# A vision block's weight preparation as steps of its attention program, with the orders of all engines written out for eight groups

## The chip, the cores and the metric

The kernel runs on one core of a Trainium2 chip. The metric is the device time of one execution in microseconds (us), the median of several runs. The core has five engines that run their own instruction streams and meet only at semaphores: PE (TensorE, matrix products and transposes), DVE (VectorE), ACT (ScalarE), POOL (GpSimd) and SP (SyncE, which here only issues DMAs). PE writes to PSUM, whose eight banks are held here in two tensors of four, `ps_s` and `ps_w`.

## The reference, cut to what matters

```python
h = tok(x)                       # 64 images of 3x112x112 -> 49 patches of 768 values
                                 #   rms norm, rounding to 8 bits, product with the token weight rounded to -1, 0, 1
                                 #   plus class token and position: h is 64 x 50 x 256
def attn(x):                     # x = layernorm(h); three scales, 16 heads of 16, causal
    for i in range(3):
        q, k, v = x @ Wq[i].T + bq[i], x @ Wk[i].T + bk[i], x @ Wv[i].T + bv[i]
        w = softmax(mask(q k^T * 4))
        o_i = layernorm((w v) @ Wo[i].T + bo[i]) * g[i] + b[i]
    return layernorm(concat(o_i) @ Wout.T + bout) * g2 + b2
h = h + attn(layernorm(h))
h = h + ffn(layernorm(h))        # gate and up 256 -> 704, silu, down 704 -> 256, all rounded to 8 bits
return h                         # the rounding steps of ffn are maxima over the WHOLE input
```

The maxima over the whole input mean that no FFN product can begin before the attention of the last image is done.

## The kernel before, in words

The program has three blocks, one after the other, each of which ends only when every engine has finished its part.

**Preparation (lines 303 to 510).** The weights are loaded into staging tensors (`tok_st`, `st_out`, `st_o`, `st_q`, `st_k`, `wv_sb`) and turned into what attention reads. The token weight is rounded and transposed (`tokT`). Wq and Wk are cut into a high part and a rest (`qk_hi`, `qk_lo`) so that PE can multiply them at a higher rate. Wo is centred (L417 to L421), transposed (L472), and multiplied with Wout (L487), so that one product later gives both the vector whose variance is wanted and the part of the final sum; this pair is `oy_hi`, `oy_lo`. The rows of biases (`brow_s`) are cut into three bf16 rows of `bias3` by a chain between ACT and POOL on one partition (L342 to L361). Nothing of the images is touched here.

**Attention (lines 697 to 1165).** The 64 images are eight groups of eight; a group is four pairs p = 0 to 3 of two images. The steps of a group are:

- for each pair: `sums` (the pair's largest value and sum of squares, L730 and L930), `scale`, `shift` (rounding, L744 and L950), `turn_q` (transposes, L1063 and L760), `embed` (token product, L1071, and statistics, L958 to L963), `norm_x` (L972), `turn_x` (transposes, L1078, and the copies `xh`, `xf` and the rest `xl`, L773 and L855);
- then, three scales each: `k` and `q` (L1087), `v` (L1104), `spread` (POOL lays k out by heads, L864), `scores` (L1125), `max`, `soft`, `sum`, `over` (the softmax), `turn_p` (L1139), `heads` (L1150), `project` (L1163), and `mix`, `mix2` (both layer norms of the end and the statistics for the FFN).

The first product `k` of a group needs the `xl` of all four pairs. `x_in` and `x_t` hold two pairs and one pair, so the load of pair 3 is issued once `x_q` of pair 1 has been written. The order on each engine is a table, `AT`: for each step its place in a round of 100 ticks, plus 100 for each round of lag behind the first steps. The same body is then run for every group (`round_parts`), with steps left out where the group does not exist. The four banks of `ps_w` go round in PE's order (`bank_plan`). Each step waits for what it needs, so the tables change only when things happen. The steps `sums`, `shift` and `turn_q` of the rounds after group 7 prepare the FFN's weights.

**FFN (lines 1229 to 1487).** It is the same in both kernels.

Of the kernel before, what the change touches and what calls it, by code (L numbers as in the profile page):

```python
# [14 lines left out]
F32 = mybir.dt.float32  # L15
# [52 lines left out]
ROUND = 100  # L68
AT = {
    "sp": {  # L70
        "sums": (0, 1, 2, 3,),
    },
    "act": {
        "sums": (9, 10, 29, 42,),
        "shift": (16, 22, 48, 62,),
# [11 lines left out]
        "sums": (1, 4, 18, 29,),
        "embed": (21, 36, 41, 51,),
        "turn_x": (50, 52, 54, 55,),
        "spread": (103, 105, 106, 108, 112, 113, 114, 119, 123, 125, 132, 140,),  # L90
        "sum": (115, 117, 120, 126, 130, 135, 139, 142, 148, 149, 207, 210,),
        "project": (131, 133, 137, 146, 147, 153, 200, 202, 209, 211, 227, 228,),
        "mix": (216, 222, 234, 238,),
        "mix2": (224, 243, 244, 245,),
    },
    "dve": {
        "sums": (3, 9, 25, 46,),
        "scale": (7, 12, 42, 62,),
        "shift": (10, 15, 53, 70,),
        "embed": (13, 36, 73, 92,),  # L100
        "norm_x": (81, 84, 90, 100,),
        "max": (114, 118, 126, 128, 138, 143, 149, 156, 169, 176, 182, 193,),
        "soft": (116, 119, 127, 130, 140, 147, 154, 161, 171, 177, 183, 202,),
        "sum": (122, 131, 134, 135, 144, 158, 164, 172, 174, 187, 191, 211,),
        "over": (129, 133, 137, 139, 148, 163, 167, 175, 178, 189, 204, 217,),
        "heads": (155, 157, 179, 188, 205, 232,),
        "project": (160, 165, 168, 185, 186, 201, 206, 208, 220, 223, 250, 252,),
# [31 lines left out]
USES_BANK = ("turn_q", "embed", "turn_x", "k", "q", "v", "turn_p", "heads", "project")


GU_CHUNKS = 2 * FC // 3


def round_parts(engine):

    body = engine_order(engine)

    def exists(step, i):
        m = i + step[-1]  # L150
        if step[0] in ("sums", "shift", "turn_q") and m >= GROUPS:
            return PAIRS * (m - GROUPS) + step[1] < (GU_CHUNKS + KC if step[0] == "sums" else GU_CHUNKS)
        return 0 <= m < GROUPS

    part = lambda i: [s for s in body if exists(s, i)]
    return [(0, part(0), 1), (1, part(1), 1), (2, body, GROUPS - 2)] + [(i, part(i), 1) for i in range(GROUPS, GROUPS + 4)]


def bank_plan():
# [4 lines left out]

    def fills(steps):
        return [(s, a) for s in steps if s[0] in USES_BANK for a in range(2 if s[0] == "turn_p" else 1)]

# [1364 lines left out]
```

## Time and profile before

| | us |
|---|---|
| median of 3 runs | 847.66 (845.89 to 847.9) |
| the profiled execution | 845.34 |
| its span in the trace | 843.5 |

The rows quoted further down come from that one profiled execution. Its span is 1.84 us shorter than its time. In a timeline row the first number is the start in us from the start of the span, the second the busy time of the row (neighbouring instructions of the same kind are merged, "xcount"), then engine, line, operation and tensors, and in brackets how long the engine had been idle and what ended that. PEclk is the clock that TensorE was granted, 1.00 being 2.4 GHz and 0.50 being 1.2 GHz.

### The profile page before, as it was taken

How to read it: one execution, taken by the hardware profiler on the slowest of the kernel's cores; microseconds unless marked ns; L12 is line 12 of the kernel's file. 1: busy time of each engine (PE TensorE's matmuls, PEld its weight loads, DVE VectorE, ACT ScalarE, POOL GpSimd, SP SyncE). 2: the span in 40 equal slices, each digit the busy share in tenths (PEclk: the TensorE clock that was granted, in tenths of full speed). 3: DMA queues.
4: the chain of work that ended last, by engine and by line, in shares of the span. 5: the costliest groups of instructions: out<-in, count | busy, mean ns of one | idle time of the engine just before them, and what ended most of it. 6: DMA issues, size and time to landing. Idle time of an engine off the chain costs nothing. (4 is left out here: it accounts for less than half of the span.)

```text
span 843.5 us, 28434 instructions
## 1 busy us (share of the span) xinstructions
PE 727.0 (86%) x11302; PEld 576.0 (68%) x11302; DVE 648.5 (77%) x1362; ACT 512.0 (61%) x1078; POOL 535.1 (63%) x806
## 2 busy tenths in 40 slices
PE   2603799999999999999999999999999999367665
PEld 0402678887888878878888877888788877234354
DVE  6535586688879887987898798879886985758847
ACT  0444566675676666666666766676666665278673
POOL 0062685596779678966977696789678763521154
PEclk9855699999999999999999999999999999879968
DMA  7001001000000000000001000000001010000004
GB/s 248 0 28 44 30 17 32 2 31 17 19 14 19 17 17 31 3 18 16 31 2 32 2 32 17 17 17 17 21 19 37 2 37 3 1 1 0 0 25 132
DMA packets 14963, 22.05 MB, mean 26 GB/s; under 512 B 1972, under 2 KB 11446, under 8 KB 14839
## 3 DMA queue, kind: packets, MB, share of 16 engines
q1 hardware_dynamic: 14402, 19.91, 7.6%
q8 instruction: 89, 1.46, 0.7%
q10 hardware_dynamic: 436, 0.40, 0.2%
q14 instruction: 36, 0.29, 0.1%
HBM read 17.03 MB, written 3.28 MB: 24 GB/s over the span
## 5 line engine op out<-in xcount | busy, mean ns | idle before, releaser
L864 POOL TENSOR_TENSOR k_bd<-kT,rmask 128x400 f32<-128x400 f32 x192 | 166.2, 891 | 13.8 <-ACT kT L780 13.1
L873 POOL TENSOR_TENSOR prob<-prob,rsum 128x400 f32<-128x400 f32 x96 | 118.6, 1235 | 20.5 <-DVE rsum L997 20.4
L810 ACT COPY pT<-ps_w 128x400 f32<-128x400 f32 x192 | 86.6, 507 | 40.4 <-PE ps_w L1139 39.8
L1139 PE MATMUL ps_w<-pack,prob 128*128 128x128 f32 x768 | 102.6, 277 | 1.8 <-POOL prob L873 1.0
L1104 PE MATMUL ps_w<-wv_sb,xf 128*50 128x128 f32 x1536 | 98.9, 272 | 0.0
L1139 PEld LDWEIGHTS ps_w<-pack,prob 128*128 128x128 f32 x768 | 84.9, 141 | 18.0 <-issue 11.2
L1163 PE MATMUL ps_w<-oy_hi,o_hi 128*128 128x512 f32 x192 | 93.8, 489 | 0.0
L795 ACT COPY v_bd<-ps_w 50x512 f32<-50x512 f32 x96 | 55.7, 581 | 47.0 <-PE ps_w L1104 45.8
L824 ACT ACTIVATE ps_w<-ps_w 128x256 f32<-128x256 f32 x96 | 35.4, 369 | 80.1 <-PE ps_w L1163 79.9
L1104 PEld LDWEIGHTS ps_w<-wv_sb,xf 128*50 128x50 f32 x1536 | 78.0, 125 | 0.3
L802 ACT ACTIVATE prob<-prob 128x400 f32<-128x400 f32 x96 | 68.0, 708 | 15.6 <-DVE prob L985 15.5
L878 POOL TENSOR_TENSOR ln<-ln,ln_eps 128x1 f32<-128x1 f32 x96 | 19.0, 198 | 92.0 <-ACT ps_w L824 92.0
L981 DVE TENSOR_REDUCE nmax<-ps_s 128x16 f32<-128x400 f32 x96 | 72.6, 757 | 5.8 <-PE ps_s L1125 5.2
L1163 PE MATMUL ps_w<-oy_lo,o_hi 128*128 128x512 f32 x192 | 76.0, 396 | 0.0
L1163 PE MATMUL ps_w<-oy_hi,o_lo 128*128 128x512 f32 x192 | 75.6, 394 | 0.0
L985 DVE TENSOR_TENSOR prob<-ps_s,nmax 128x400 f32<-128x400 f32 x96 | 74.0, 771 | 1.1
L992 DVE TENSOR_REDUCE rsum<-prob 128x16 f32<-128x416 f32 x96 | 73.5, 773 | 1.3 <-ACT prob L802 1.2
L1087 PE MATMUL ps_w<-xh,qk_hi 128*128 128x400 f32 x192 | 70.6, 368 | 1.7 <-POOL xl L855 1.7
L1125 PE MATMUL ps_s<-k_bd,qT 64*25 64x200 f32 (+1 forms) x3072 | 70.5, 291 | 0.0
L1087 PE MATMUL ps_w<-xl,qk_hi 128*128 128x400 f32 x192 | 67.0, 349 | 0.0
L1087 PE MATMUL ps_w<-xh,qk_lo 128*128 128x400 f32 x192 | 66.7, 348 | 0.0
L1013 DVE SCALAR_TENSOR_TENSOR acc<-ps_w,ln,acc 128x256 f32<-128x256 f32 x64 | 30.9, 482 | 42.9 <-POOL ln L880 33.7
(214 smaller groups left out, 1766.6 us busy)
## 6 DMA issues: line engine op xcount, KB each, us to landing
x_in<-in_x SPq DMA_DIRECT2D x64, 147.0 KB
out<-hidden SPq DMA_DIRECT2D x16, 200.0 KB
tok_st<-in_tok_w SPq DMA_DIRECT2D x1, 768.0 KB, 7.2
st_out<-in_wout SPq DMA_DIRECT2D x1, 768.0 KB, 5.2
st_o<-in_wo SPq DMA_DIRECT2D x1, 768.0 KB, 7.0
st_q<-in_wq SPq DMA_DIRECT2D x1, 768.0 KB, 8.7
st_k<-in_wk SPq DMA_DIRECT2D x1, 768.0 KB, 10.1
wv_sb<-in_wv SPq DMA_DIRECT2D x1, 768.0 KB, 10.3
```

The costliest lines, as they stand in the source:

```text
L802: nc.scalar.activation(pr, pr, ACT.Exp).then_inc(exp_ready, 1)
L810: nc.scalar.copy(pT[:, s % 2, 4 * a:4 * a + 4, :, e * LQ:(e + 1) * LQ], ps_w[:, bank].rearrange("p (j t) -> p j t", j=4)[:, :, 0:QB * LQ]. ...
L864: last = nc.gpsimd.tensor_tensor(k_bd[:, v % KBD, c], kT[:, w % 2, c, 2 * p * L:(2 * p + 2) * L].unsqueeze(1).broadcast_to([P, HR, 2 * L]) ...
L873: nc.gpsimd.tensor_tensor(pr, pr, rsum[:, s % 2, e, 1].unsqueeze(2).broadcast_to([P, H, WIDTH[e]]), ALU.mult).then_inc(prob_ready, 1)
L981: nc.vector.tensor_reduce(top, s_ps, AX.X, ALU.max, negate=True).then_inc(max_ready, 1)
L985: nc.vector.tensor_tensor(prob[:, s % 2, e, :, 0:WIDTH[e]].rearrange("p (r h) t -> p r h t", r=2), s_ps, top.unsqueeze(3).broadcast_to([P, ...
L992: nc.vector.tensor_reduce(rsum[:, s % 2, e, 0], prob[:, s % 2, e, :, 0:WIDTH[e] + 1], AX.X, ALU.add).then_inc(sum_ready, 1)
L1087: mm = nc.tensor.matmul(G[:, 0:GT], wt[:, w, q, k, c * P:(c + 1) * P], xt[:, k], start=(t == 0), stop=(t == 3 * KC - 1))
L1104: mm = nc.tensor.matmul(G[row:row + L, cols], xf[:, k, tokens], wv_sb[:, w, k, e], start=False, stop=(k == KC - 1), skip_group_check=True)
L1125: mm = nc.tensor.matmul(ps_s[32 * b:32 * b + LQ, e, r, c * HR * W:(c + 1) * HR * W], qT[rows, w % 2, c, first:first + LQ], k_bd[rows, v % ...
L1139: mm = nc.tensor.transpose(G[:, j * P:(j + 1) * P], flat[:, (4 * a + j) * P:(4 * a + j + 1) * P], pack[:])
L1163: mm = nc.tensor.matmul(G[:], ot[:, s % 2, c, 2 * (p % 2):2 * (p % 2) + 2].rearrange("p b t -> p (b t)"), wt[:, w, c], start=False, stop=( ...
```

## The change

The block of preparation is gone. Its operations are now steps in the tables of the attention block (`tok_sum`, `tok_turn`, `beta`, `y_scale`, `o_centre`, `wo_turn`, `fold`, `k_hi`, `q_lo`, `v_cut`, `z_cut` and more), placed among the steps of group 0. The first two pairs of images are issued right behind the token weight and the identity, ahead of all other weights. Since preparation and attention now live at the same time, the staging tensors are laid into tensors that are used late: `st_out`, `st_o`, `st_q` and `woT` into `hidden` from slot 8 on (group 2 and later), `st_k` into `k_bd`, the token weight into `pT`, the bias rows into `wgT`, `wdT` and `acc`.

Four operations move to another engine: the scaled shift of the token weight from DVE to ACT, the copies of `tokT` from DVE to ACT (two instead of six), the rest of Wk from DVE to POOL, and the memsets from DVE to POOL. The bias cut is made in two pieces, one for v (768 values) and one for the output (1536 values), instead of 2304 values at once. `AT` now lists a tick for each step of each of the eight groups, so groups may differ in order; `round_parts`, `Part` and the loop of SP are gone. Waits are added where a step of attention first needs something prepared (`qk_cut` before `k` and `q`, `v_cut` before `v`, `o_cut`, `fold_lo` and `z_cut` before `project`, `tok_copied` before `embed`, `fold_lo` before group 2's `embed`).

```diff
-    with nc.Block() as block:
-        @block.sync
-        def _(sp):
-            sp.dma_start(tok_st[:], tok_w.rearrange("(k p) n -> p k n", p=P)).then_inc(loads["tok"], 16)
...
-    prep.close()
+    st_out, st_o, st_q = (hidden[:, 8 + 6 * j:14 + 6 * j] for j in range(3))
+    woT = hidden[:, 26:32].rearrange("p a (b t) -> p (a b) t", t=P).rearrange("p (s d e) t -> p s d e t", s=NS, d=KC)
...
+                if kind == "weights" and step[1] == 1:
+                    sp.dma_start(st_q, weight_rows(wq)).then_inc(loads["wq"], 16)
+                    sp.dma_start(st_k, weight_rows(wk)).then_inc(loads["wk"], 16)
...
+                if kind == "k_lo":
+                    pool.wait_ge(split_k, 1)
+                    nc.gpsimd.tensor_tensor(qk_lo[:, :, 1], by_row(st_k), qk_hi[:, :, 1].bitcast(F32), ALU.subtract).then_inc(qk_cut, 1)
...
+                if kind == "q_lo":
+                    dve.wait_ge(split_q, 1)
+                    nc.vector.tensor_tensor(qk_lo[:, :, 0], by_row(st_q), qk_hi[:, :, 0].bitcast(F32), ALU.subtract).then_inc(qk_cut, 1)
...
+                if kind == "fold":
+                    s = step[1]
+                    pe.wait_ge(scaled_y, 1)
+                    pe.wait_ge(wo_copied, s + 1)
+                    wait_released(pe, step)
...
                 if kind in ("k", "q"):
                     w, c, q = *step[1:3], int(kind == "k")
                     pe.wait_ge(xl_ready, PAIRS * (m + 1))
+                    pe.wait_ge(qk_cut, 2)
...
                     pe.wait_ge(o_lo_ready, S * m + s + 1 + AHEAD)
+                    pe.wait_ge(o_cut, 1)
+                    pe.wait_ge(fold_lo, NS)
+                    pe.wait_ge(z_cut, 3)
...
-ROUND = 100
...
+    "pe": {
+        "tok_mean": (0,),
+        "turn_q": (1, 4, 8, 9, 25, 38, 60, 68, 92, 111, 128, 144, 163, 175, 194, 214, 240, 260, 275, 290, 307, 322,
```

**SP, from its first instruction.** `x_in` is the buffer of images, L623 in the changed kernel; the four loads of the first two pairs now stand third. In the kernel before, SP reads:

```order
L306 DMA tok_st<-in_tok_w 128x2x768
L307 DMA id<-in_ident 128x128
...
L313 DMA st_q<-in_wq 128x6x256
L313 DMA st_k<-in_wk 128x6x256
L314 DMA wv_sb<-in_wv 128x6x256
L303 UNCONDITIONAL_BRANCH
L698 UNCONDITIONAL_BRANCH
L714 DMA x_in<-in_x 49x768 x16
```

and in the changed kernel:

```order
L591 DMA pT<-in_tok_w 128x2x768
L592 DMA id<-in_ident 128x128
L623 DMA x_in<-in_x 49x768 x4
...
L601 DMA hidden<-in_wq 128x6x256
L602 DMA k_bd<-in_wk 128x6x256
L604 DMA wv_sb<-in_wv 128x6x256
L605 DMA pT<-in_brow 1x768
L606 DMA hidden<-in_wout 128x6x256
L607 DMA hidden<-in_wo 128x6x256
L608 DMA acc<-in_brow 1x1024
L623 DMA x_in<-in_x 49x768 x60
```

The first two pairs moved from behind everything to the front; pairs 2 and 3 of group 0 are the first of the sixty loads behind the weights.

**PE, up to the first product `k` of group 0** (`xh` with `qk_hi`). The kernel before has, after its block of preparation:

```order
L1063 MATMUL ps_w<-id,x_q 128x128 x6
L1071 MATMUL ps_w<-tokT,x_qT 128x256 x6
L1063 MATMUL ps_w<-id,x_q 128x128 x6
L1078 MATMUL ps_w<-id,x_t 128x128 x2
L1071 MATMUL ps_w<-tokT,x_qT 128x256 x6
L1078 MATMUL ps_w<-id,x_t 128x128 x6
L1087 MATMUL ps_w<-xh,qk_hi 128x400
```

The changed kernel has:

```order
L1247 MATMUL ps_w<-tokT,x_qT 128x256 x12
L1185 MATMUL ps_w<-hidden,bcol 1x256 x6
L1238 MATMUL ps_w<-id,x_q 128x128 x12
L1247 MATMUL ps_w<-tokT,x_qT 128x256 x6
L1220 MATMUL ps_w<-ybias,ones 128x256
L1214 MATMUL ps_w<-ones,wgT 128x1 x6
L1255 MATMUL ps_w<-id,x_t 128x128 x2
L1247 MATMUL ps_w<-tokT,x_qT 128x256 x6
L1255 MATMUL ps_w<-id,x_t 128x128 x6
L1229 MATMUL ps_w<-hidden,bo_col 1x256 x6
L1265 MATMUL ps_w<-xh,qk_hi 128x400
```

`beta` (L1185), `y_spread` (L1220), `bo_turn` (L1214) and `bo_fold` (L1229) moved in among the transposes and token products of group 0. `wo_turn` and `fold` stand further down, behind the first scores.

**DVE, between the last shift of group 0 and the first maximum** (`nmax`). The changed kernel has, among group 1's first steps:

```order
L957 TENSOR_TENSOR qk_lo<-hidden,qk_hi 128x3x512
L1029 TENSOR_REDUCE xs<-x_in 128x1
...
L1049 TENSOR_SCALAR x_q<-x_t 128x768
L967 TENSOR_REDUCE o_mean<-hidden 128x6
L969 TENSOR_SCALAR o_mean<-o_mean 128x6
L971 TENSOR_TENSOR hidden<-hidden,o_mean 128x1536
L1085 TENSOR_REDUCE nmax<-ps_s 128x16 x2
```

In the kernel before, the same work (`st_o` and `o_mean`) stands in the block of preparation:

```order
L417 TENSOR_REDUCE o_mean<-st_o 128x6
L419 TENSOR_SCALAR o_mean<-o_mean 128x6
L421 TENSOR_TENSOR st_o<-st_o,o_mean 128x1536
L426 TENSOR_REDUCE b_mean<-brow_st 1x3
L428 TENSOR_SCALAR b_mean<-b_mean 1x3
```

The centring of Wo and the rest of Wq moved to where DVE formerly waited for the first scores.

## Rows read from the trace of the kernel before

**Rows 1.** The page: the span, and PE's clock in 40 slices.
```profile
span 843.5 us, 28434 instructions
...
PEclk9855699999999999999999999999999999879968
```

**Rows 2.** Windows: busy us (and count) by engine, clock, DMA share, GB/s.
```profile
40.00:50.00 10.00, 0.00 (x0) 0.00 (x0) 4.83 (x1) 6.69 (x4) 4.54 (x1) 0.65 0.00 0
...
180.00:260.00 80.00, 79.72 (x1349) 65.40 (x1349) 67.76 (x153) 51.88 (x117) 61.60 (x99) 1.00 0.06 18
```

**Rows 3.** Waits of PE, 93 to 720 us: total us, times, longest.
```profile
PE ps_s L1116 <- POOL k_bd L864: 1.7, 6, 0.5
PE ps_s L1116 <- DVE prob L985: 1.4, 2, 1.2
```

**Rows 4.** Timeline: the token weight is taken up; the first images are asked for.
```profile
7.99 1.75 DVE L376 TENSOR_REDUCE tok_sum<-tok_st 128x2 f32<-128x1536 f32 x1 [5.06 <-DMA tok_st<-in_tok_w]
...
58.56 15.78 SPq L714 DMA_DIRECT2D x_in<-in_x  x8
```

**Rows 5.** Timeline: group 0 from its first image to its first scores.
```profile
62.38 0.84 ACT L730 ACTIVATE x_t<-x_in 128x768 f32<-128x768 f32 x1 [4.08 <-DMA x_in<-in_x]
...
73.13 0.56 DVE L950 TENSOR_SCALAR x_q<-x_t 128x768 bf16<-128x768 f32 x1
...
77.41 0.84 ACT L730 ACTIVATE x_t<-x_in 128x768 f32<-128x768 f32 x1 [1.98 <-DMA x_in<-in_x]
...
93.00 0.70 PE L1087 MATMUL ps_w<-xh,qk_hi 128*128 128x400 f32 x1 [1.71 <-POOL xl L855]
...
102.97 0.26 PE L1116 MATMUL ps_s<-mask,pick 64*128 64x200 bf16 x2
```

**Rows 6.** DMA: a window of the weights; images alone, 58 to 80 us.
```profile
10.00:20.00 10.00, 4.91 (x14) 1.76 (x14) 7.94 (x23) 0.43 (x3) 0.00 (x0) 0.96 1.09 354
```
```profile
GB/s 0 0 56 101 179 162 184 162 162 78 11 0 0 30 0 0 0 0 0 0 0 123 106 128 168 22 0 0 0 0 84 134 151 173 6 0 0 0 0 0
```

**Rows 7.** Timeline: operations of preparation that move into attention.
```profile
12.52 4.35 PE L465 MATMUL ps_w<-st_out,bcol 128*1 128x256 f32 x12 [1.88 <-DMA st_out<-in_wout]
...
16.98 1.66 DVE L414 TENSOR_SCALAR st_out<-st_out,gcol 128x256 f32<-128x256 f32 x6 [1.18 <-PE ps_w L465]
...
22.31 0.93 DVE L426 TENSOR_REDUCE b_mean<-brow_st 1x3 f32<-1x768 f32 x1
...
22.54 2.79 PE L472 MATMUL ps_s<-id,st_o 128*128 128x128 f32 x12 [5.67 <-DVE st_o L421]
...
28.21 5.40 PE L487 MATMUL ps_s<-st_out,woT 128*128 128x256 f32 x24
...
33.54 1.49 PE L495 MATMUL ps_s<-one_row,brow_s 1*128 1x1 f32 x12
...
35.50 1.89 PE L505 MATMUL ps_w<-st_out,bo_col 128*1 128x256 f32 x8
...
39.65 2.11 ACT L342 CAST bias<-brow_s 1x2304 bf16<-1x2304 f32 x1 [5.41 <-DVE brow_s L452]
41.67 1.47 ACT L344 CAST qk_hi<-st_k 128x1536 fp32r<-128x1536 f32 x1
```

**Rows 8.** Timeline: the same subtraction on DVE, alone and beside POOL.
```profile
35.15 1.75 DVE L444 TENSOR_TENSOR qk_lo<-st_q,qk_hi 128x1536 fp32r<-128x1536 f32 x1
...
41.84 4.54 POOL L359 TENSOR_TENSOR brow_r<-brow_s,bias 1x2304 f32<-1x2304 f32 x1 [39.72 <-ACT bias L342]
43.16 4.83 DVE L454 TENSOR_TENSOR qk_lo<-st_k,qk_hi 128x1536 fp32r<-128x1536 f32 x1 [3.55 <-ACT qk_hi L344]
```

**Rows 9.** Timeline: the end of attention and the first FFN instruction.
```profile
724.08 0.39 PE L1158 MATMUL ps_w<-bias,ones 96*128 96x512 bf16 x1 [1.29 <-DVE o_lo L1003]
...
735.61 0.17 DVE L1045 COPY stat<-ln 128x4 f32<-128x4 f32 x1
...
736.86 1.28 ACT L1242 ACT_TABLE_LOAD   x1 [8.86 <-PEq L697]
```

More of the change, by code:

```diff
@@ L85 @@
     },
     "pool": {
[L87 to L94, printed above, removed]
+        "sums": (0, 1, 2, 3, 16, 17, 28, 36, 57, 59, 69, 78, 109, 114, 121, 137, 168, 172, 184, 186, 221, 227, 236,
+            259, 281, 291, 303, 305, 338, 339, 353, 365,),
@@ L100 @@
[L100 to L107, printed above, removed]
@@ new lines @@
+        "fold": (53, 54, 55,),
+        "heads": (56, 57, 74, 80, 102, 115, 123, 127, 145, 146, 174, 185, 201, 202, 215, 219, 246, 261, 262, 277,
+            284, 295, 320, 321, 346, 347, 358, 365, 386, 403, 413, 424, 425, 436, 455, 470, 480, 492, 503, 507, 534,
+            540, 552, 561, 570, 577, 587, 588,),
+        "project": (61, 62, 63, 64, 93, 96, 97, 98, 113, 114, 124, 126, 134, 135, 136, 137, 156, 157, 158, 159, 180,
[4 rows of a table added]
+    },
+}
+PER_GROUP = {
+    "sums": PAIRS, "scale": PAIRS, "shift": PAIRS, "turn_q": PAIRS, "embed": PAIRS, "norm_x": PAIRS, "turn_x": PAIRS,
+    "mix": PAIRS, "mix2": PAIRS, "k": NS * KC, "q": NS * KC, "v": S, "heads": S, "spread": V, "project": V,
+    "scores": U, "max": U, "soft": U, "sum": U, "over": U, "turn_p": U,
@@ L139 @@
[L139 to L156, printed above, removed]
@@ L191, in layer @@
+USES_BANK = ("tok_mean", "tok_turn", "beta", "wo_turn", "fold", "bo_turn", "y_spread", "bo_fold",
+             "turn_q", "embed", "turn_x", "k", "q", "v", "turn_p", "heads", "project")
+def bank_plan():
+    order = [(step, a) for step in engine_order("pe") if step[0] in USES_BANK for a in range(2 if step[0] == "turn_p" else 1)]
+    return {key: (n % NBANK, n // NBANK + 1, order[n - NBANK] if n >= NBANK else None) for n, key in enumerate(order)}
 def layer(nc, x, tok_w, cls, pos, wq, wk, wv, wo, bq, bk, brow, ln_g, ln_b, wout, ln2_g, ln2_b,
@@ L668, in layer, with walk @@
+    def walk(engine, do):
+        for step in engine_order(engine):
+            do(step)
     HALVES = ((0, 0), (ROWB, 1))
@@ L720, in _ @@
         def _(act):
-            def do(step, part):
-                kind, m = step[0], part.group(step)
+            for dst, src in ((token0, pos), (g2, ln2_g), (b2, ln2_b)):
+                act.dma_start(dst[:], src.broadcast_to([P, D])).then_inc(loads["small"], 16)
+            act.wait_ge(pool_up, 1)
+            for row in (0, ROWB):
+                act.dma_start(cls_st[row:row + 1], cls).then_inc(loads["small"], 16)
+            act.wait_ge(set_up, 1)
+            act.sem_inc(pt_read, AHEAD)
```

937 lines of the change are left out of this document (534 added, 403 removed), and 69 rows, old and new, of the table AT.

## The prediction

> **What bounds the kernel now.** I read the page's slices first, then windows of the stages, PE's waits, and last the timelines at the two ends of attention. Three stretches appear. Up to about 93 us PE is mostly idle: in the window from 40 to 50 us it does nothing while ACT, DVE and POOL cut bias rows [rows 2], and its clock is at the lower level in slices 3 and 4 [rows 1]. From then on PE is busy 79.72 of 80 us in a window of the middle, with DVE at 67.76 as the next [rows 2], and its waits from 93 to 720 us are a few of up to 1.2 us [rows 3]: this stretch lasts as long as PE has work. Last, attention drains and the FFN follows: its first instruction stands at 736.86 us [rows 9], and from there to the end of the span, 843.5 [rows 1], is 106.6 us of code that the change leaves alone.
>
> So the time is the start of the first product `k` (93.00 us [rows 5]), plus PE's work, plus drain and FFN. I call that start T. The change pays by moving T forward, and costs by what it adds to PE's work behind T, and by waits that new orders open.
>
> **T before.** The first images are asked for when preparation is over, at 58.56 us [rows 4]. The first pair is taken up at 62.38 [rows 5]. Pair 3 can only be loaded once pair 1's `x_q` is written, at 73.13 + 0.56 = 73.69, and is taken up at 77.41, 3.7 us later; from there to T it is 93.00 - 77.41 = 15.6 us of a chain from engine to engine [rows 5].
>
> **T after, the data.** Pairs 0 and 1 are issued behind the token weight, pairs 2 and 3 behind all weights. Ahead of pair 2 on the queue stand the token weight and five more loads of 768 KB, 64 KB of identity, 384 KB of broadcast rows (from ACT's queue) and 588 KB of the first two pairs: 5.64 thousand KB, or 5.8 MB. Weights came at 354 GB/s [rows 6], which makes 16.4 us; with a start at about 4 us that is 20. Images do not come at that rate: loaded alone they moved 162 to 184 GB/s at the most [rows 6]. For the first two pairs that costs 3.5 us instead of 1.7, for pairs 2 and 3 (another 588 KB) 3.5 us. Pair 3 is then there at about 25 us, not before 23. The condition of before (`x_q` of pair 1 plus 3.7 us) lies earlier: the token weight is there at 7.99 us [rows 4], and two pairs through `sums`, `scale` and `shift` take 73.69 - 62.38 = 11.3 us [rows 5], which gives 8 + 11.3 + 3.7 = 23.
>
> The Trainium skill (DMA: Bandwidth & Descriptors, Why a DMA increments its semaphore by 16 and not by 1) says that a load is spread over the largest number of engines up to 16 that divides its slowest dimension, so 49 rows would go to 7 of 16. The trace agrees: 7/16 of 354 GB/s would be 155. The same page (Queues, rings and completion order) has descriptors taken in ring order on each engine, so that pairs 2 and 3 would wait for the weights. No row of before has images queued behind weights. If that rule did not hold here, pair 3 would come at 23 us, and T and the time would be 2 us less.
>
> **T after, what is put into the chain.** From the landing of pair 3 to T the tables now also have, on PE, `beta` 4.35, `bo_turn` 1.49 and the larger part of `bo_fold` 1.89 = 7.7 us; on DVE the centring of the bias rows (two operations of some 0.93) and `y_scale` 1.66 = 3.5 us; on ACT two casts of 1.47 and three bf16 cuts of 768 values, one third of 2.11 each, = 5.0 us [rows 7]. Together 16.2 us. All exposed would be the upper bound, none (hidden in the waits of the chain, as the 1.98 us of ACT before pair 3 or the 1.71 us of PE before `k` [rows 5]) the lower. `bo_fold` stands right ahead of `k` and is nearly bare, `beta` stands ahead of two transposes that pairs 2 and 3 need; the casts of ACT stand between `sums` and `shift`. I take half, 8.1 us. `q_lo`, 1.75 us alone [rows 8], runs on DVE while PE, ACT and POOL finish the last `turn_x`, and I cost it at nothing; bare it would be 1.75.
>
> The rest of Wk moves to POOL. DVE's subtraction of 128x1536 took 1.75 us alone and 4.83 us when it began during POOL's operation, which ended at 41.84 + 4.54 = 46.38: up to that moment 3.2 us, and then its own 1.6 [rows 8]. So DVE stood still while POOL worked. POOL's `k_lo` and `v_left` now run beside DVE's part of the chain. I add 1.5 us for it, between 0 and 3.1. The Trainium skill (SBUF — State Buffer, SBUF: two separate sides) states this as a rule against such a mix: the port pair that GpSimd shares with VectorE is held for a whole instruction, and the other blocks. The trace agrees; by it alone, every POOL subtraction of the preparation would cost DVE up to its full length.
>
> T after = 25 + 15.6 + 8.1 + 1.5 = 50.2 us, 42.8 us earlier. Bounds: 23 + 15.6 + 2 = 41, and 27 + 15.6 + 16.2 + 1 = 60.
>
> **PE's work behind T.** `wo_turn` (2.79) and `fold` (5.40) [rows 7] now stand among scores and products of group 0, where PE is full, so they cost 8.2 us in whole. At the full clock throughout the transposes may take 1 us less. All other products are the same in number and shape. PE begins `k` at the lower clock as before, so that term cancels.
>
> **New waits behind T.** DVE has `o_centre` right ahead of the first maximum. In the kernel before the first scores come 102.97 - 93.00 = 10 us after T [rows 5], and in that time DVE now has `q_lo` and some 8 us of work; `o_centre` ends about 11 us after T. The last rows of `bias3` hang on a chain of ACT and POOL, and `fold_lo` on ACT and DVE; `project` waits for all of them, behind `fold`, `heads` and `v`. POOL has 3 us of subtraction in the middle of the spreads (1536 of 2304 values, 4.54 us [rows 8]). I take 2 us in all. Above, one such subtraction bare and a late `project` give 8 (3.0, and the 5.40 of `fold` once more as the time by which its rest could be late [rows 7]); below, the waits of 1.7 and 1.4 us [rows 3] could vanish in the new orders, -3.
>
> **The drain.** Before, PE's last two projections begin at 724.08 and the last statistics end at 735.78 [rows 9], 11.7 us. The new order transposes the last four probabilities in one go, then does both heads, then the last four projections, so four pairs instead of two go through `mix` and `mix2` after PE, which makes DVE's tail longer; but PE has about 10 us more work left behind the last scores, and waits less for them. I set the sum at nothing, plus or minus 3.
>
> **The sum.** 845.34 - 42.8 + 8.2 + 2 = 812.7 us for an execution like the profiled one. The median of the runs of before lies 2.3 us above that execution; I add 1.3 and predict 814.
>
> **The rivals.**
> 1. The start pays in full: DVE's and PE's additions hide in the idle parts, T is 41 to 45, and orders per group take away the small waits of PE. 845.3 - 50 + 8.2 - 2 = 801.5. For it: the chain of before has waits on each engine [rows 5] in which additions can hide. Against: the three additions stand on three different engines of one chain. From 796 to 805.
> 2. The start stays late: preparation is then itself the chain, as a walk with the additions bare, T 57 to 62. 845.3 - 34 + 8.2 + 5 = 824.5. This is also the case that the change does not do what it says: `k` waits for the preparation, not for the images. For it: ACT, PE and DVE each do the preparation in series with the images. From 820 to 832.
> 3. The new orders take PE's cover away in every group, and the kernel gets slower. The tables now pair the steps (two maxima, then two exponents). The scores of a bank wait until DVE has read the last ones; the longest such wait was 1.2 us [rows 3]. There are six pairs of scores in each of eight groups, 48 places. At 1.2 us in each it costs 58 us, and the time is 845.3 - 42.8 + 10.2 + 58 = 871. It decides from 32.6 / 48 = 0.68 us at each place. Against it: DVE is busy 67.76 of 80 us [rows 2], which leaves 12 us in each group, so that a table would have to be placed badly for it.
>
> **How the numbers follow.** The forecast, 805 to 820, has a chance of 0.6; rival 1, 0.17; rival 2, 0.17; rival 3 in full 0.03, and in part (a gain of which less than half is left, 832 to 845) 0.03. The range reaches to both sides until about 0.2 is out: 799 to 827. About 0.3% is what a measurement of this kernel can tell from no change, 2.5 us here. Faster by over that: 0.96; within it: 0.01; slower: 0.03.
>
> **What would show each step.** In the profile after, the first product `k` stands at about 50 us; the fourth `sums` of ACT begins at about 25 us after a wait for the DMA of `x_in`; PE in the stretch behind T is as dense as before, but for `fold`, whose rows add 8 us between T and the start of the FFN: attention then takes 737 - 93 + 10 = 654 us from T on. FFN is 107 us in both. The prediction is wrong if the fourth `sums` comes later than 28 us (the data), if from there to T it is more than 32 us (the chain), or if T to the start of the FFN is over 662 us or under 647 (the orders).

## The result and the profile after

| | before | predicted | after |
|---|---|---|---|
| median of the runs (4 and 4) | 847.78 | 814 (799 to 827) | 819.58 (819.25 to 823.28) |
| profiled execution | 845.34 | 812.7 | 819.57 |
| fourth `sums` of ACT begins | 77.41 | 25 | 28.97 |
| from there to the first product `k` (T) | 15.6 | 25.2 | 26.8 |
| T | 93.00 | 50.2 | 55.75 |
| T to the first FFN instruction | 643.9 | 654 | 656.4 |
| from there to the end of the span | 106.6 | 106.6 | 105.5 |

All in us. The ratio of the runs is 0.9683, with a 95% interval of 0.9654 to 0.9712: faster, by 27 us (28 between the medians). The rows account for the profiled executions: T came 37.2 us earlier, attention from T on took 12.5 us longer, the FFN 1.1 us less, together 25.8 us, and the two executions differ by 25.77. The median is inside the range, 5.6 us above the number. The profiled execution is 6.9 us above its own number: T is 5.5 late, the stretch from T to the FFN 2.4 longer than forecast, the FFN 1.1 shorter.

The page after: the span, and PE's clock in 40 slices, which answers to [rows 1].
```profile
span 817.7 us, 28887 instructions
...
PEclk9869999999999999999999999999999999679979
```

The timeline after, from the load of Wo to the first product `k`, which answers to [rows 5, 7]. First the start in us, then the busy time.
```profile
14.75 2.06 SPq L607 DMA_DIRECT2D hidden<-in_wo  x1
...
28.97 0.84 ACT L707 ACTIVATE x_t<-x_in 128x768 f32<-128x768 f32 x1 [0.74 <-DMA x_in<-in_x]
...
33.52 3.43 POOL L834 TENSOR_TENSOR qk_lo<-k_bd,qk_hi 128x1536 fp32r<-128x1536 f32 x1
...
35.23 1.74 DVE L979 TENSOR_SCALAR b_mean<-b_mean 1x3 f32<-1x3 f32 x1
...
36.90 1.63 POOL L841 TENSOR_TENSOR pT<-pT,bias 1x768 f32<-1x768 f32 x1
37.04 2.30 DVE L981 TENSOR_TENSOR wgT<-acc,b_mean 1x768 f32<-1x768 f32 x1
...
39.27 0.54 DVE L1049 TENSOR_SCALAR x_q<-x_t 128x768 bf16<-128x768 f32 x1
...
42.93 2.55 PE L1214 MATMUL ps_w<-ones,wgT 1*128 1x1 f32 x12
...
45.90 1.49 PE L1247 MATMUL ps_w<-tokT,x_qT 128*128 128x256 bf16 x6
...
50.45 2.28 DVE L957 TENSOR_TENSOR qk_lo<-hidden,qk_hi 128x1536 fp32r<-128x1536 f32 x1
...
51.07 2.12 POOL L864 TENSOR_TENSOR xl<-xf,xh 128x200 fp32r<-128x200 f32 x1
51.20 4.32 PE L1229 MATMUL ps_w<-hidden,bo_col 128*1 128x256 f32 x12
...
55.75 0.45 PE L1265 MATMUL ps_w<-xh,qk_hi 128*128 128x400 f32 x1 [0.23 <-POOL xl L864]
```

The rows show three things. Pair 3 is taken up at 28.97, waited for until then. Between the `shift` of pair 3 on ACT (which ends at 34.03) and its `x_q` on DVE at 39.27 stands only the centring of the bias rows, and two of its operations take 1.74 and 2.30 us while POOL subtracts. At the end `xl`, 0.60 us elsewhere, takes 2.12 beside DVE's `q_lo`; four `xl` and the additions between them then end just where `k` begins.

Behind T, in group 0, POOL begins a subtraction (`z_left`) 0.4 us before DVE's `x_q` of group 1's second pair. What follows, on POOL, DVE and PE:
```profile
68.96 3.10 POOL L841 TENSOR_TENSOR wgT<-wgT,bias 1x1536 f32<-1x1536 f32 x1
...
69.35 5.42 DVE L1049 TENSOR_SCALAR x_q<-x_t 128x768 bf16<-128x768 f32 x1
...
79.86 1.09 PE L1194 MATMUL ps_w<-id,hidden 128*128 128x128 f32 x4 [2.75 <-DVE hidden L1062]
```

Windows of the start of `k` before (93 to 100 us) and after (55.75 to 62.75), and of the stretch behind the wait. Columns: PE, PEld, DVE, ACT, POOL busy, then the granted clock.
```profile
93.00:100.00 7.00, 7.00 (x27) 6.96 (x28) 2.61 (x7) 3.50 (x7) 3.07 (x5) 0.66 0.00 0
```
```profile
55.75:62.75 7.00, 6.48 (x38) 6.17 (x39) 5.83 (x11) 4.61 (x7) 7.00 (x9) 1.00 0.00 1
```
```profile
75.00:80.00 5.00, 1.86 (x53) 1.20 (x48) 4.77 (x10) 4.30 (x7) 4.38 (x6) 0.83 0.19 60
80.00:85.00 5.00, 5.00 (x45) 3.42 (x46) 4.87 (x10) 3.91 (x7) 2.43 (x3) 0.50 0.02 3
```

`x_q` takes 5.42 instead of 0.56 us, `embed` on DVE is late, the bank that `wo_turn` wants is late, PE idles 2.75 us, and then its clock is at the lower level (1.2 GHz) for five microseconds. At T it is the other way round: before, PE had idled 1.71 us ahead of `k` and ran it at the lower level for two thirds of 7 us; after, PE is busy with `bo_fold` until 0.23 us ahead of `k`, and `k` runs at 2.4 GHz at once. The end, PE's last product and the first FFN instruction, first before:
```profile
727.10 0.39 PE L1163 MATMUL ps_w<-oy_hi,o_lo 128*128 128x512 f32 x1
```

and after:
```profile
698.88 0.39 PE L1350 MATMUL ps_w<-oy_hi,o_lo 128*128 128x512 f32 x1
...
712.16 1.28 ACT L1429 ACT_TABLE_LOAD   x1 [11.69 <-PEq L588]
```
From the end of PE's last projection to the first FFN instruction it is 12.9 us, where it was 9.4.

### The profile page after: what moved, and what is told of

Its sections match the earlier page's. It is cut to its first block and busy times, and to the rows that moved or that the text cites. A ratio compares the mean times of both kernels' runs of the same rounds, so it can differ in the third digit from the quotient of the medians.

```text
span 817.7 us, 28887 instructions
## 1 busy us (share of the span) xinstructions
PE 728.1 (89%) x11302; PEld 573.7 (70%) x11302; DVE 649.7 (79%) x1346; ACT 519.0 (63%) x1085; POOL 544.5 (67%) x817
## 5 line engine op out<-in xcount | busy, mean ns | idle before, releaser
L1323 PE MATMUL ps_w<-pack,prob 128*128 128x128 f32 x768 | 95.1, 275 | 1.8 <-DVE hidden L1062 0.9
L891 POOL TENSOR_TENSOR ln<-ln,neg_half 128x1 f32<-128x1 f32 x96 | 53.4, 557 | 7.5
```

Of the source, the lines that this page charges most:

```text
L1323: mm = nc.tensor.transpose(G[:, j * P:(j + 1) * P], flat[:, (4 * a + j) * P:(4 * a + j + 1) * P], pack[:])
```

## The experiments

The first four were timed side by side, then four, two and two more, each lot with the kernel before on the same chip (846.11, 846.05, 846.66 and 847.92 us). "T to FFN" is from the first product `k` to the first FFN instruction in the profiled execution. Where steps move, a table `MOVES` is added which `engine_order` applies: each entry is a step and the step that it now stands behind.

| run | median us | ratio, interval | fourth `sums` | T | T to FFN |
|---|---|---|---|---|---|
| c0_after | 820.58 | 0.9696 (0.9671 to 0.9721) | 28.98 | 55.75 | 655.9 |
| e1_data | 815.53 | 0.9630 (0.9601 to 0.9659) | 26.67 | 53.45 | 655.9 |
| e2_klo | 821.48 | 0.9698 (0.9671 to 0.9726) | 28.83 | 55.80 | 658.5 |
| e3_zleft | 821.25 | 0.9683 (0.9657 to 0.9710) | 29.35 | 56.13 | 659.1 |
| e4_fold_twice | 824.86 | 0.9735 (0.9711 to 0.9759) | 29.14 | 55.92 | 660.9 |
| e5_before_x | 848.01 | 1.0012 (0.9998 to 1.0027) | 77.70 | 93.79 | |
| e6_behind | 823.61 | 0.9733 (0.9708 to 0.9757) | 29.37 | 52.56 | 663.8 |
| e7_tail | 816.97 | 0.9660 (0.9635 to 0.9684) | 29.01 | 55.91 | 651.5 |
| e8_rests | 815.41 | 0.9633 (0.9619 to 0.9648) | 29.15 | 55.28 | 650.0 |
| e9_best | 814.36 | 0.9619 (0.9606 to 0.9633) | 29.60 | 54.12 | 651.5 |
| e10_chain | 810.26 | 0.9557 (0.9539 to 0.9575) | 26.35 | 50.55 | 653.6 |
| e11_data_rests | 812.98 | 0.9593 (0.9576 to 0.9610) | 26.20 | 51.61 | 654.8 |

**The changed kernel again.**

> The changed kernel once more, as a reference for the runs beside it on the same chip. Theory and rival alike expect 819.6 us (within 2.5), the first product k at 55.75 us, the fourth sums of ACT at 28.97 us, the first FFN instruction at 712.2 us.

It reproduced the rows shown above within 0.1 us up to 75 us, the 5.4 us of `x_q` included (5.41), and T to FFN within 0.5. The wait of 2.75 us came again, but the lower clock behind it was shorter: 0.66 from 80 to 85 us, that is 3.4 us at half speed, where it had been 0.50 throughout.

**Weights behind the images.**
```diff
-        "weights": (2, 3, 4,),
+        "weights": (2, 3, 4, 6.5,),
...
+                if kind == "weights" and step[1] == 3:
+                    sp.dma_start(st_o, weight_rows(wo)).then_inc(loads["wo"], 16)
+                    sp.dma_start(wv_sb[:].rearrange("p s k e n -> p (s k) (e n)"), weight_rows(wv)).then_inc(loads["wv"], 16)
```

> The loads of Wo and Wv (1.5 MB) move on the DMA queue behind the images of pairs 2 and 3. Theory (the images of pair 3 are late by 4 us because they stand behind all weights in the queue, and the whole chain up to T starts with them): 1.5 MB at 354 GB/s are 4.4 us; the fourth sums of ACT begins at about 24.5 instead of 28.97 us, T at 51.3 instead of 55.75, time 815.2. Rival 1 (the images are late for another reason, such as their issue after x_q of pair 1): the fourth sums stays within 1 us of 28.97 and the time at 819.6. Rival 2 (data are early but the chain is bound by ACT, DVE and POOL work of the preparation): the fourth sums moves by 4 us and T by less than 2, time above 817.6.

The timeline of that run, ACT and PE:
```profile
24.96 0.80 ACT L738 COPY x_qT<-ps_w 128x768 bf16<-128x768 bf16 x1 [2.33 <-DVE ln L1066]
...
26.67 0.84 ACT L708 ACTIVATE x_t<-x_in 128x768 f32<-128x768 f32 x1
...
53.45 0.45 PE L1266 MATMUL ps_w<-xh,qk_hi 128*128 128x400 f32 x1 [0.78 <-POOL xl L865]
```
The fourth `sums` moved by 2.3 us and T by exactly as much, so the chain from there on is rigid, and both rivals fall. But 4.4 us had been expected. `sums` no longer waits for a DMA: it stands on ACT behind the copy `x_qT` of pair 1, which waits for pair 0's statistics. So the data were worth 2.3 us, and the next bound, the work of the first two pairs, stood right behind them. The profiled executions differ by 2.1 us (816.34 against 818.48), the medians by 5.0. The intervals of the two ratios just fail to overlap, so part of the rest may be real; it has no row in the trace, and its cause stays open.

**The rest of Wk on DVE.**
```diff
-        "k_lo": (6,),
...
+        "k_lo": (29.5,),
```

> The rest of Wk (k_lo, 128x1536) is subtracted on DVE right behind q_lo instead of on POOL at 33.5 us. Theory (DVE stands still beside POOL's subtraction, so b_centre's second and third operation take 1.74 and 2.30 us instead of 0.17 and 0.95, and x_q of pair 3 waits for them): those two fall to below 2.0 us together, x_q of pair 3 is written 1.5 to 2.9 us earlier than at 39.27, and T comes 1.5 us earlier at 54.2, if k_lo's 1.75 us on DVE hide beside the rest of bo_fold. Time 818.1. Rival (the long operations of DVE have another cause): the two stay at about 4 us and T at 55.75 or later, by up to 1.75.

The timeline of DVE, POOL and PE:
```profile
36.94 0.94 DVE L981 TENSOR_TENSOR wgT<-acc,b_mean 1x768 f32<-1x768 f32 x1
37.81 0.54 DVE L1049 TENSOR_SCALAR x_q<-x_t 128x768 bf16<-128x768 f32 x1
...
51.19 2.16 DVE L954 TENSOR_TENSOR qk_lo<-k_bd,qk_hi 128x1536 fp32r<-128x1536 f32 x1
...
51.69 2.24 POOL L863 TENSOR_TENSOR hidden<-hidden,b 128x256 f32<-128x256 f32 x1
...
55.80 0.45 PE L1265 MATMUL ps_w<-xh,qk_hi 128*128 128x400 f32 x1 [1.73 <-POOL xl L861]
```
The subtraction moved to DVE with its step. That of `b_centre` fell from 2.30 to 0.94 us, and `x_q` came 1.5 us earlier, so POOL's work did hold DVE. Its other operation stayed long (1.77), beside `v_left`. The gain did not reach T: `k_lo` on DVE now holds POOL's addition (0.73 elsewhere) for 2.24 us among the `xl`, and PE waits for them. The same 1.5 us were paid at the other end, from DVE to POOL. The expected 54.2 for T and 818.1 for the time failed.

**The first subtraction of the output rows later.**
```diff
+MOVES = {
+    "pool": ((('z_left', 0, 0), ('sum', 3, 0)),),
+}
```

> POOL's first subtraction of the output bias rows (1x1536, 3.10 us at 68.96) moves behind its first four normalisations of probabilities, some 15 us later. Theory (x_q of group 1's second pair, 0.56 us alone, took 5.42 us at 69.35 because POOL's operation held DVE, all of DVE and the bank of embed came late, PE stood idle for 2.75 us and then ran from 80 to 85 us at the lower clock): x_q takes less than 2.6 us, PE has no wait over 1 us between 70 and 90 us and no stretch at the lower clock there, and the time from T to the FFN falls from 656.4 to about 652, time 815.6. Rival (the wait comes from the order of the steps on PE and DVE): x_q gets shorter, but the wait and the lower clock stay, time 819.6.

DVE, POOL and PE:
```profile
69.71 0.88 DVE L1059 TENSOR_SCALAR x_q<-x_t 128x768 bf16<-128x768 f32 x1
...
83.90 3.10 POOL L851 TENSOR_TENSOR wgT<-wgT,bias 1x1536 f32<-1x1536 f32 x1
...
84.28 2.74 DVE L1068 TENSOR_TENSOR xs<-xs,tok_unit 128x1 f32<-128x1 f32 x1
...
88.82 0.26 PE L1309 MATMUL ps_s<-mask,pick 64*128 64x200 bf16 x2 [2.21 <-issue]
...
99.95 0.92 PE L1344 MATMUL ps_w<-pT,v_bd 128*32 128x50 f32 x64 [1.94 <-DVE oy_lo L1009]
```
`x_q` took 0.88 us and PE was busy all of 70 to 80 us: the wait of 2.75 us and the lower clock behind it were gone, as expected. But nothing was left of it at the end (T to FFN 659.1), and the expected absence of any wait over 1 us up to 90 us failed. The subtraction now held an operation of one column for 2.74 us and stood ahead of two spreads (86.97 to 88.62), and PE's scores came behind them, after 2.2 us of idling for which the profile names no releaser. At 99.95 PE waited 1.94 us more for a late `oy_lo`, and its clock was 0.66 from 100 to 105 us. In group 1, PE idled another 1.60 us at 203.35, again without a releaser. So the holding of `x_q` is shown, and the expected 815.6 failed, since the subtraction did other harm at its new place.

**`fold` twice.**
```diff
-                    for k in range(KC):
+                    for k in (0, 1, 0, 1):
                         for kk in range(KC):
                             mm = nc.tensor.matmul(G[:, k * D:(k + 1) * D], woT[:, s, kk, k], st_out[:, s * KC + kk],
```

> PE makes the products of fold twice (24 more matrix products of 128x256, same result). Theory (work of PE behind T is bare, so what the change added there costs its full length): the row of fold grows from 5.3 to 10.6 us and the time by 5.3, to 825.4 against 820.1 for the changed kernel. Rival (behind T there is slack, and added work of PE partly disappears in waits that exist anyway): the time grows by less than 3 us.

The row of `fold` grew from 5.34 to 10.52 us, T to FFN by 5.0 us, the median by 4.3. Work of PE behind T is bare.

**The kernel before with its first images loaded at once.**
```diff
+            sp.wait_ge(x_clear, 1)
+            for p in (0, 1):
+                for row, b in ((0, 0), (ROWB, 1)):
+                    sp.dma_start(x_in[row + 1:row + L, p, :], x[2 * p + b]).then_inc(x_loaded[p], 16)
             for n in ("wk", "wv"):
```

> The kernel before, with one part of the change alone: the images of the first two pairs are loaded behind the weights during the preparation, not after it. Theory (they only spare their own landing; the rest of the gain comes from preparation running beside group 0): the first sums of ACT begins at 58.7 instead of 62.38 us, T at 89.3 instead of 93.00, time 843.6 less than 1 us off, against 847.3 for the kernel before (ratio 0.996). Rival (loading at once is the main part): T falls by 10 us or more.

ACT and DVE:
```profile
59.57 0.84 ACT L737 ACTIVATE x_t<-x_in 128x768 f32<-128x768 f32 x1 [0.47 <-PEq L305]
...
65.38 0.95 DVE L937 TENSOR_REDUCE xs<-x_in 128x1 f32<-128x768 f32 x1 [3.75 <-POOL prob L901]
```
and in the kernel before:
```profile
64.58 0.95 DVE L930 TENSOR_REDUCE xs<-x_in 128x1 f32<-128x768 f32 x1 [3.76 <-POOL prob L894]
```
The first `sums` on ACT came 2.8 us earlier, and T did not move forward (93.79). The images were not what group 0 waited for longest: in both kernels DVE's first reduction waits for POOL's memsets at the start of the attention block. This part alone is worth nothing here; the gain needs the preparation and group 0 to overlap. No run has the overlap without the early images.

**The centring, `bo_turn` and `bo_fold` behind T.**
```diff
+MOVES = {
+    "pe": ((('bo_turn', 0, 0), ('q', 1, 0, 0)), (('bo_fold', 0, 0), ('bo_turn', 0, 0)), (('bo_fold', 1, 0), ('bo_fold', 0, 0)),),
+    "dve": ((('b_centre', 0, 0), ('q_lo', 0, 0)), (('bo_col', 0, 0), ('shift', 0, 1)), (('z_row', 0, 0), ('bo_col', 0, 0)), (('z_row', 1, 0), ('z_row', 0, 0)),),
+}
```

> The centring of the bias rows, bo_turn and bo_fold (DVE 5.0 us as measured, PE 2.6 and 4.3 us) move behind the first products k and q; y_scale, the casts and POOL's subtractions stay. Theory (these stand bare in the chain from the images to T: x_q of pair 3 waits 4.9 us for the centring, embed of pair 3 waits 2 us for bo_turn): x_q of pair 3 at 34.4 instead of 39.27 us, T at 48.8 instead of 55.75, and 3 to 4 us of it are given back behind T where PE is full, so T to the FFN is 659 to 660 instead of 656.2, time 816.7. Rival (POOL is the real chain: its subtraction k_lo, v_left and the memset of prob end at 40.9 us, and its work on the second layer norm comes behind them): x_q of pair 3 is early, but T stays at 53 or later and the time is 820 or more.

DVE and PE, and the window behind T:
```profile
35.94 1.82 DVE L1060 TENSOR_SCALAR x_q<-x_t 128x768 bf16<-128x768 f32 x1 [1.21 <-ACT x_qT L748]
...
52.56 0.70 PE L1276 MATMUL ps_w<-xh,qk_hi 128*128 128x400 f32 x1 [5.20 <-POOL xl L875]
...
62.13 2.75 PE L1240 MATMUL ps_w<-hidden,bo_col 128*1 128x256 f32 x12 [0.30 <-issue]
```
```profile
52.56:59.56 7.00, 7.00 (x27) 6.95 (x28) 4.26 (x11) 3.13 (x5) 5.20 (x7) 0.67 0.00 1
```
T came 3.2 us earlier, not 7: `x_q` was itself held beside `k_lo` (1.82 us), and POOL kept the rest. And 7.9 us came back behind T: the moved products (`bo_turn` 1.49, `bo_fold` 2.75), and a start of `k` at the lower clock (0.67 over 7 us, 2.3 us lost), with PE idle for 5.20 us ahead of it. The run was 3 us slower than the changed kernel. What stands ahead of `k` on PE, in the shadow of POOL's `xl`, costs nothing there, and `k` behind it started at the higher level.

**The end in the order of before.**
```diff
+    "pe": ((('heads', 4, 7), ('turn_p', 9, 7)), (('project', 8, 7), ('turn_p', 10, 7)), (('project', 9, 7), ('project', 8, 7)),),
...
+    "dve": ((('mix', 0, 7), ('project', 8, 7)), (('project', 9, 7), ('mix', 0, 7)), (('heads', 5, 7), ('project', 9, 7)), (('mix', 1, 7), ('heads', 5, 7)),),
```

> The last group's end in the order of the kernel before: the heads and projections of the fifth scale half (pairs 0 and 1) come ahead of the last transposes and heads. Theory (four pairs instead of two go through both layer norms on DVE after PE's end, and DVE is full from there on): DVE's first sum of the last four begins 1.2 us earlier than at 695.91, PE's end to the first FFN instruction falls from 12.9 us towards the 9.4 of before, time 2 to 3 us less than the changed kernel's 820.1. Rival (the drain is the same sum of work in either order): within 1 us of 820.1.

POOL and DVE in group 0, and the end:
```profile
68.60 0.88 DVE L1062 TENSOR_SCALAR x_q<-x_t 128x768 bf16<-128x768 f32 x1
...
69.03 3.43 POOL L854 TENSOR_TENSOR wgT<-wgT,bias 1x1536 f32<-1x1536 f32 x1
...
697.53 0.39 PE L1363 MATMUL ps_w<-oy_hi,o_lo 128*128 128x512 f32 x1
...
707.41 1.28 ACT L1442 ACT_TABLE_LOAD   x1 [8.29 <-PEq L601]
```
```profile
690.00:697.90 7.90, 5.87 (x81) 4.25 (x82) 6.06 (x18) 1.91 (x7) 3.23 (x8) 0.78 0.01 3
```
The drain is 9.5 us again, as before, but from the first `k` of group 7 to the FFN it is 102.8 us against 101.7: what the drain gave, PE's stretch ahead of it took. From that `k` to PE's end PE idled 3.4 us, where it had idled 0.9, and its last 8 us ran at a clock of 0.78. The rival holds for the end. The 3.6 us of the median come from elsewhere. In this execution, with not one step of group 0 changed, `x_q` happened to start 0.43 us ahead of `z_left`; it took 0.88 us, the wait of PE did not arise, and group 0 took 69.2 instead of 74.4 us. The runs of this kernel lie from 814.19 (the profiled one) to 819.99. PE's wait of 2.75 us stands in the traces of after, c0_after, e1_data, e2_klo, e4_fold_twice and e6_behind (2.74), and not in this one. That the same near tie decides the runs without a trace is likely and not shown.

**All subtractions on DVE.**
```diff
-        "k_lo": (6,),
-        "v_left": (7, 18,),
-        "z_left": (24, 37,),
...
+MOVES = {
+    "dve": ((('k_lo', 0, 0), ('q_lo', 0, 0)), (('v_left', 0, 0), ('norm_x', 0, 0)), (('v_left', 1, 0), ('sums', 1, 1)), (('z_left', 0, 0), ('soft', 5, 0)), (('z_left', 1, 0), ('max', 7, 0)),),
+    "act": ((('z_cut', 2, 0), ('fold_hi', 2, 0)),),
+}
```

> All five subtractions that cut weights and bias rows (k_lo, v_left twice, z_left twice) run on DVE, none on POOL; nothing else moves. Theory (a subtraction on POOL and work on DVE hold each other, and whether group 0 loses 4 to 5 us depends on which of the two starts first, z_left or the x_q of DVE): the operations of b_centre take 0.2 and 1.0 us instead of 1.74 and 2.30, x_q of group 1's second pair less than 1.5 us instead of 5.42, PE has no wait over 1 us between 60 and 95 us, T at 54 to 56 us (k_lo now ends beside POOL's xl), T to the FFN 651 to 653 instead of 656, time 815 and without two levels among the runs. Rival (DVE is full in this stretch, so 7 us more work on it cost more than the holding did): T to the FFN stays at 655 or more, time 819 or more.

DVE's centring, `x_q`, and PE's window:
```profile
35.41 0.16 DVE L990 TENSOR_SCALAR b_mean<-b_mean 1x3 f32<-1x3 f32 x1
35.64 0.94 DVE L992 TENSOR_TENSOR wgT<-acc,b_mean 1x768 f32<-1x768 f32 x1
...
67.99 0.88 DVE L1060 TENSOR_SCALAR x_q<-x_t 128x768 bf16<-128x768 f32 x1
```
```profile
75.00:80.00 5.00, 5.00 (x65) 4.24 (x63) 4.97 (x8) 4.87 (x10) 3.08 (x3) 1.00 0.01 3
```
The rows came as expected: 0.16 and 0.94, 0.88, no wait of PE over 0.7 us from 60 to 95 us, T 55.28, T to FFN 650.0, median 815.41. DVE has some 8 us more work and the kernel is 5 us faster than the changed one. `x_q` of pair 3 came at 36.52 instead of 39.27, and T gained only 0.5 us of that: beside `q_lo` and `k_lo` on DVE an `xl` took 2.12 and an addition 2.24 us on POOL. Only the spread of the runs (812.57 to 817.24) did not shrink.

**The chain rearranged, twice.** Both have the edits of e1_data and e8_rests, and all four `xl` of group 0 ahead of the additions to `hidden`. The first of the two also put POOL's memsets ahead of the work on the images, `k_hi` and `k_lo` into the pause before pair 3, `q_lo` and the centring behind `embed` and `norm_x`, and `bo_turn` behind the last `embed`.
```diff
+    "dve": ((('k_lo', 0, 0), ('embed', 0, 0)), (('y_row', 0, 0), ('shift', 3, 0)), (('norm_x', 0, 0), ('y_row', 0, 0)), (('b_centre', 0, 0), ('norm_x', 0, 0)), (('q_lo', 0, 0), ('embed', 2, 0)), (('y_scale', 0, 0), ('norm_x', 3, 0)), (('bo_col', 0, 0), ('norm_x', 3, 0)), (('v_left', 0, 0), ('norm_x', 0, 0)), (('v_left', 1, 0), ('sums', 1, 1)), (('z_left', 0, 0), ('soft', 5, 0)), (('z_left', 1, 0), ('max', 7, 0)),),
...
+    "pool": ((('clear', 0, 0), ('sums', 1, 0)), (('clear', 1, 0), ('clear', 0, 0)), (('clear', 2, 0), ('clear', 1, 0)),),
```

> As the run with all subtractions on DVE, and in addition: the loads of Wo and Wv behind the images, k_hi and k_lo in the pause before the third pair's images, the memsets early, q_lo and the centring where DVE waits for PE, bo_turn behind the last embed, and all four xl ahead of the additions to hidden. Theory (the holding and the bare steps of the chain from the images to T can be had back): fourth sums of ACT at 26.7 us, from there to T 20 to 22 us instead of 26.8, T at 47 to 49, T to the FFN 651 to 654, time 807 to 811. Rival (what leaves one engine of the chain shows on the next, as with the centring moved alone): T at 51 or later, time 813 or more.

```profile
15.09 1.80 POOL L837 MEMSET v_bd<- 128x2048 f32 x1
...
15.83 4.50 DVE L938 CAST id<-id 128x128 bf16<-128x128 f32 x1
```
T was 54.12 and not 47 to 49: the cast of the identity, 0.22 us in c0_after, took 4.50 us beside the memsets, and everything behind it moved back by 3.4 us. So the second put them elsewhere:
```diff
+    "dve": ((('k_lo', 0, 0), ('embed', 0, 0)), (('q_lo', 0, 0), ('embed', 1, 0)), (('y_row', 0, 0), ('shift', 3, 0)), (('norm_x', 0, 0), ('y_row', 0, 0)), (('b_centre', 0, 0), ('embed', 2, 0)), (('v_left', 0, 0), ('norm_x', 3, 0)), (('bo_col', 0, 0), ('norm_x', 3, 0)), (('y_scale', 0, 0), ('norm_x', 3, 0)), (('v_left', 1, 0), ('z_row', 1, 0)), (('z_left', 0, 0), ('soft', 5, 0)), (('z_left', 1, 0), ('max', 7, 0)),),
+    "act": ((('k_hi', 0, 0), ('small', 0, 0)), (('q_hi', 0, 0), ('sums', 3, 0)), (('v_cut', 0, 0), ('turn_q', 3, 0)), (('v_cut', 1, 0), ('sums', 1, 1)), (('z_cut', 2, 0), ('fold_hi', 2, 0)),),
+    "pool": ((('clear', 0, 0), ('embed', 1, 0)), (('clear', 1, 0), ('turn_x', 3, 0)),),
+    "pe": ((('bo_turn', 0, 0), ('embed', 3, 0)),),
```

> As the run with every step rearranged, but the memsets of POOL stand again behind the first images' work (ahead of them they shifted x_q of pair 1 from 20.1 to 23.5 us), q_hi and q_lo move into pauses of ACT and DVE ahead of x_q of pair 3, the centring into the pause between the last two embeds. Theory (memsets on POOL held DVE's clipping of the token weight, and the rest of the chain was moved back with it): x_q of pair 1 at 20.5, the fourth sums at 26.7, T at 49 to 51, T to the FFN 650 to 652, time 807 to 810. Rival (the chain gives nothing more): T at 53 or later, time above 812.

```profile
45.45 5.18 PE L1244 MATMUL ps_w<-hidden,bo_col 128*1 128x256 f32 x12 [1.46 <-DVE bo_col L1009]
...
50.55 0.45 PE L1280 MATMUL ps_w<-xh,qk_hi 128*128 128x400 f32 x1
```
T is 50.55, in the expected 49 to 51, the median 810.26: 0.9557 of the kernel before, the best of all, where the changed kernel had 0.9696 in c0_after. T to FFN was 653.6 and not 650 to 652; 1.60 us of it are idling of PE in group 1 (at 191.89) for which the profile names no releaser. `k` now follows `bo_fold` without a pause, 4.9 us behind the last `xl` (45.69), so `bo_fold` is the next bound.

> Two edits together: the loads of Wo and Wv behind the images, and all subtractions on DVE. Theory (the two are independent: the one moves the start of the chain by 2.3 us, the other frees group 0 of the holding): the fourth sums at 26.7, T at 53.0, T to the FFN 650, time 812.9 or 2.3 less than with the subtractions alone. Rival (they share their gain): time as with the subtractions alone, 815.

The window behind T:
```profile
51.61:58.61 7.00, 7.00 (x30) 6.95 (x30) 3.11 (x12) 3.51 (x6) 3.96 (x6) 0.76 0.00 0
```
The median is 812.98, as the sum of the two said. In the trace T moved by 3.7 us against e8_rests and T to FFN is 654.8, not 650. Of these 4.8 us the trace shows two parts: `k` began at a clock of 0.76 over 7 us, which is 1.7 us lost, and PE idled 1.60 us in group 1 (at 194.37), without a releaser. An idling of 1.60 us stands in group 1 of e2_klo, e3_zleft and e10_chain too. Why it comes in some kernels and not in others stays open, and so does the rest.

## Why the prediction was right, and where it was short

**The frame held.** The time is T, plus PE's stretch, plus drain and FFN. e1_data moved T by 2.3 us, and T to FFN did not change; e4_fold_twice added 5.2 us of work of PE, and 5.0 came through.

**The data: 25 predicted, 28.97 measured.** That is past the 28 us which the prediction itself had set as the sign that this step is wrong. The failed step is the rate. The sum divided 5.8 MB by the 354 GB/s of one window [rows 6], from 4 us on; after, the windows from 6 to 10 and 10 to 15 us move 220 and 275 GB/s. SP issued Wq only at 7.65 us, behind the first images and seven small loads; how much of the lower rate is the late issue and how much the images no run separates. Wo, issued at 14.75, landed 11.0 us later. That pairs 2 and 3 wait behind the weights was right: with 1.5 MB less ahead of them no `sums` of theirs waits for a DMA any more (e1_data), as the ring order of the Trainium skill (DMA: Bandwidth & Descriptors, Queues, rings and completion order) has it. The lower bound of 23 was short too. It started the first pair at 8 us, with the token weight, and the pair was taken up at 10.91. The first pairs' own work lets pair 3 in at 26.2 to 26.7 at best (e1_data, e10_chain, e11_data_rests), since it includes preparing the token weight.

**The chain: 25.2 predicted, 26.8 measured, for partly other reasons.** Half of the inserted work was a guess that hit. `bo_fold` was feared as bare (1.89 in [rows 7], where 8 of its 12 products stand; 4.32 here) and is hidden under POOL's `xl`. `bo_turn` is bare (it delays the last `embed` by 2 us), and the centring wholly so: 5.0 us, of which 2.0 are its own work. The step that failed is DVE standing still. It was set at 1.5 us, with 3.1 as the most; the two operations alone lost 2.9 (1.74 against 0.16, and 2.30 against 0.94 in e8_rests), and a subtraction on POOL also holds whatever else of DVE it meets. `q_lo` at nothing was wrong: its own time is covered, but it holds `xl` for 1.5 us, on the engine that sets T.

**PE's added work: 8.2 predicted, 7.7 measured** (`fold` 5.34, `wo_turn` 2.35, a third of its products at the lower clock).

**"PE begins `k` at the lower clock as before, so that term cancels": wrong.** At a granted clock of 0.66 over 7 us, 4.8 us ran at half speed, which is 2.4 us lost. The kernel before (0.66), e5_before_x (0.64) and e6_behind (0.67), which have no `bo_fold` ahead of `k`, lose them. Of the eleven traces with `bo_fold` there, ten have a clock of 1.00 over the 7 us behind T, and e11_data_rests has 0.76.

**New waits: 2 predicted.** The one that came was none of those named: the holding in group 0, 2.75 us idle and 2.5 us by the clock behind it (five microseconds at half speed; in c0_after 1.7). With all subtractions on DVE, T to FFN fell from 656 to 650. The 5.25 us of the holding, less the 2.4 of the clock at T, are 2.9: the number looks right by luck, while both parts of it were missing.

**The drain: 0 plus or minus 3 predicted.** It is 3.5 us longer behind PE's end. From group 7's first `k` to the FFN it is 101.7 us against 98.6, 3.1 more, just outside. The order of the tail alone does not explain it (e7_tail).

Together these terms make 7.7 + 5.25 - 2.4 + 3.1 = 13.65 us, where T to FFN grew by 12.5; the 1.1 between them has no row.

**The rivals.** Rival 3 did not come: PE's density in the middle is that of before (80.00 of 80 us in the window from 260 to 340). Rival 2 had T at 57 to 62; T was nearer to it than to the forecast's 50.2, for its reason in part. Rival 1 needed the additions hidden in the pauses, which e10_chain shows to be possible for part of them.

## What to carry to other kernels

When serial preparation is dissolved into a pipeline, the gain is the overlap, and it is read at the chain from the last input to the first full-rate product: list for each engine what stands in that chain, and put nothing of the preparation there except what another engine's tail covers. Work that is moved from a full engine to an idle one is not free if the two hold each other: ask which of the two operations will start first, and what waits for the loser. Work of PE right ahead of the dense stretch can be worth more than its removal: taken away, the stretch began at half speed here (e6_behind). It is no guarantee, as e11_data_rests shows, and in e10_chain the same work has become the bound.

## What the runs showed of the hardware

**POOL and DVE hold each other, and the order of starting decides.** `x_q` of 128x768, 0.56 us alone: 0.88 when it started 0.43 us ahead of POOL's subtraction, which then took 3.43 instead of 3.10; 5.42 when 0.4 us behind it. The Trainium skill (SBUF — State Buffer, Who interferes with whom) says that issue order decides who blocks, not the shape. The trace agrees.

**The loser can wait for more than one instruction.** POOL's subtraction ended at 72.06, `x_q` at 74.77; in between POOL ran its next spreads back to back (four of them from 72.03 to 77.09). In e9_best the cast of the identity stood from 15.83 to 20.33, through seven memsets of POOL in a row.

**It goes in both directions and hits small operations.** A multiplication of three numbers took 1.74 us instead of 0.16, an addition of one column on POOL 1.61 instead of 0.19 beside `q_lo` (e9_best). One sum over the free axis was not held (`b_mean` of 768 values: 0.91 beside POOL's `k_lo`, 0.91 in e8_rests).

**Half a microsecond of order is worth five.** The same steps of group 0 took 69.2 us in e7_tail and 74.4 in c0_after, two kernels whose orders differ in group 7 alone. Of the 5.2 us, 2.75 are PE's wait and 1.7 the lower clock behind it.
